# Row buffers, weighing on ScalarE, and the order of the first weights in a four-layer graph kernel on one core

## The reference, cut to what matters

```python
# layer 0: mean over neighbours, then two products and a third of their concatenation
agg = mask @ h / max(deg, 1)
out0 = relu(concat([h @ W_self + b_self, agg @ W_nb + b_nb]) @ W_comb + b_comb)
# layers 1 (8 heads of 64), 2 (4 heads of 128, quaternion weights), 3 (1 head of 512)
Wh = h @ W                                   # rows, one block of columns for each head
e = leaky_relu(f_src[i] + f_dst[j], 0.2)     # f_src, f_dst: one number for each row and head
attn = softmax(where(adj > 0, e, -9e15))
out = attn @ Wh                              # layer 2: elu(out)
```

## Time and profile before

| | us |
|---|---|
| median of three runs | 1111.23 |
| lowest and highest of them | 1106.15, 1111.57 |
| the profiled execution, whole | 1109.11 |
| its span in the trace | 1106.9 |
| busy: TensorE, VectorE, GpSimd, ScalarE | 844.4, 774.2, 634.1, 430.3 |

### The profile page before, as it was taken

One profiled execution on the slowest core, in us unless ns is written; L12 is line 12 of the kernel. 1 busy time (PEld: TensorE's weight loads), 2 busy tenths in 40 slices (PEclk: granted clock), 3 DMA queues, 4 the chain that ended last, 5 costly groups with the idle time before them and its releaser, 6 DMA issues. The chain is left out here.

```text
span 1106.9 us, 11271 instructions
## 1 busy us (share of the span) xinstructions
PE 844.4 (76%) x2786; PEld 471.1 (43%) x2786; DVE 774.2 (70%) x2327; ACT 430.3 (39%) x1277; POOL 634.1 (57%) x636
## 2 busy tenths in 40 slices
PE   0889869999928745959999989467799928876354
PEld 0344434433317534835666646244444523332121
DVE  3899986943349839938689995477899825646374
ACT  3677868111115423624554334355663511110000
POOL 5003401667767777437776730677777057777772
PEclk9999989999959986988999999898999959997767
DMA  9998998938878898647887841678778267776761
GB/s 358 413 395 336 386 393 251 324 104 267 267 248 285 284 233 284 202 153 214 246 245 209 227 128 47 177 232 239 222 211 229 72 155 205 203 206 196 199 189 73
DMA packets 87599, 257.49 MB, mean 233 GB/s; under 512 B 18694, under 2 KB 22182, under 8 KB 83433
## 3 DMA queue, kind: packets, MB, share of 16 engines
q0 software_dynamic: 46896, 157.18, 49.3%
q1 hardware_dynamic: 33116, 85.89, 21.1%
q10 hardware_dynamic: 7516, 13.63, 3.5%
HBM read 209.81 MB, written 53.66 MB: 238 GB/s over the span
## 5 line engine op out<-in xcount | busy, mean ns | idle before, releaser
L1148 POOL DMA_INDIRECT arena<-T,arena x476 | 497.7, 1046 | 266.5 <-issue 202.8
L771 PE MATMUL psum<-arena,misc 128*128 128x512 f32 x408 | 207.3, 630 | 32.9 <-DVE arena L1527 25.4
L747 PE MATMUL psum<-arena 128*128 128x264 f32 (+1 forms) x832 | 207.8, 394 | 0.9 <-ACT arena L869 0.9
L670 PE MATMUL psum<-misc,arena 128*128 128x128 f32 (+1 forms) x520 | 87.3, 294 | 153.6 <-ACT arena L853 93.0
L747 PEld LDWEIGHTS psum<-arena 128*128 128x128 f32 (+1 forms) x832 | 159.5, 195 | 59.3 <-issue 25.6
L1527 DVE TENSOR_TENSOR arena<-arena 128x512 f32<-128x512 f32 x238 | 157.4, 689 | 1.2
L670 PEld LDWEIGHTS psum<-misc,arena 128*128 128x128 f32 (+1 forms) x520 | 65.2, 150 | 198.3 <-ACT arena L853 109.5
L853 ACT ACTIVATE arena<-arena 128x512 f32<-128x512 f32 x104 | 85.0, 818 | 114.8 <-DVE arena L1405 70.0
L822 PE MATMUL psum<-arena 128*128 128x512 f32 (+1 forms) x208 | 110.3, 679 | 19.2 <-ACT arena L866 19.2
L771 PEld LDWEIGHTS psum<-arena,misc 128*128 128x128 f32 x408 | 75.4, 200 | 103.5 <-issue 66.8
L869 ACT ACTIVATE arena<-psum 128x128 f32<-128x128 f32 (+1 forms) x312 | 82.3, 283 | 88.8 <-PE psum L670 88.7
(11 more groups left out here) (143 smaller groups left out, 972.5 us busy)
## 6 DMA issues: line engine op xcount, KB each, us to landing
arena<-in_adj SPq DMA_DIRECT2D x25, 1663.5 KB, 12.4
T<-arena SPq DMA_DIRECT2D x75, 260.0 KB, 3.8
arena<-T,arena POOLq DMA_INDIRECT x476, 4.2
T<-arena ACTq DMA_DIRECT2D x25, 256.0 KB, 9.4
XV<-in_x SPq DMA_DIRECT2D x1, 6400.0 KB, 29.8
XV<-arena ACTq DMA_DIRECT2D x25, 256.0 KB, 3.8
PW<-arena POOLq DMA_DIRECT2D x5, 1024.0 KB, 27.0
arena<-in_x SPq DMA_DIRECT2D x1, 3072.0 KB, 18.7
```

The lines of the kernel that those rows point to most:

```text
L670: last = e.transpose(to[:, k * P:k * P + n], src[0:n, k * P:(k + 1) * P], ident[0:n, 0:n])
L747: last = e.matmul(p_wh[m % 2][0:n, a, :], ht[:, k, 0:n], WL[l][:, k, a, :], start=k == 0, stop=k == 3)
L771: e.matmul(p_num[s % 3].rearrange("p (a o) -> p a o", a=2), ident, halves(GB[:, BASE[l, s] + of[n][0], :])[:, :, 0:HALF], start=n == 0, st ...
L1148: e.indirect_dma_start(GB[:, BASE[l, s] + k, 0:ROW], None, dr["T"][l], bass.IndirectOffsetOnAxis(ap=(IDP if l else IDX)[:, t, k:k + 1], ax ...
```

## The change

Five edits go together.

1. From layer 1 on the rows for the next table lie in four buffers instead of two (`ROWS`: `WO` and the first two of `XV`, which are free by then), and the stores count on four semaphores.
2. In layer 2 ScalarE multiplies the last rows of a tile by their weights (`aid`, after `node_ht` and before `exp` in its round), one [128 x 128] activation for each of the four heads: 4 rows of the tile with 15 slots, 2 of each with 8 or 7, 1 of each with 6, 5 or 4. That is 22 of 119 rows and 88 activations. TensorE waits for them on a semaphore of their own, and VectorE before it overwrites the weights.
3. ScalarE does `turn(0)` between `mark(0)` and `mark(1)`, and `mix(0, 0)` and `mix(0, 1)` between `mark(1)` and `mark(2)`. SyncE issues the second piece of adj ahead of the 2 KB load of b_nb.
4. The five copies into `PW` and that of the bias go from GpSimd's queue to SyncE's, behind the loads of the attention vectors (after the second-last mark) and ahead of the copy of x into `XV`, of the places and of the load of the lists.
5. VectorE's product of 2048 columns (L1353, six times) becomes four of 512.

```diff
+def aided(l, t):
+    return {15: 4, 8: 2, 7: 2, 6: 1, 5: 1, 4: 1}.get(SLOTS[t], 0) if l == 2 else 0
+def aided_ahead(l, s):
+    return sum(aided(i, t) for i in range(1, l + 1) for t in (ORDER if i < l else ORDER[:s]))
...
+    ROWS = WO + [v[:, 0:WIDE] for v in XV[0:2]]
...
+    def row_buffer(l, s):
+        return WO[s % 2] if l == 0 else ROWS[s % 4]
     def wait_stored(e, l, s):
-        e.wait_ge(S[f"stored{s % 2}"], 16 * (l * NT // 2 + s // 2 + 1))
+        e.wait_ge(S[f"stored{s % 4}"], 16 * (l * len(range(s % 4, NT, 4)) + s // 4 + 1))
...
+        load_adj(1)
         e.dma_start(g["bcol"], dr["b_nb"].rearrange("(k p) -> p k", p=P), allow_slow_non_contiguous=True).then_inc(S["bcol0"], 16)
-        load_adj(1)
...
+        for which in range(5):
+            src = (W0[0], W0[1], S2, PB, S1)[which]
+            if which == 0:
+                e.wait_ge(S["bank_out"], bank("mix", 1, 3) + 1)
+            elif which == 2:
+                e.wait_ge(S["w1"], 8 * 16)
+            elif which == 3:
+                e.wait_ge(S["hamilton"], 16)
+            elif which == 4:
+                e.wait_ge(S["bank_out"], bank("turn", 3, 3) + 1)
+            e.dma_start(dr["PW"][which], src.rearrange("p k o -> p (k o)")).then_inc(S[f"pw{which}"], 16)
+        e.wait_ge(S["bias_row"], 1)
+        e.dma_start(dr["PB"], g["brow"][0:1, 0, :]).then_inc(S["pb_out"], 16)
...
-                buf = WO[s % 2]
+                buf = row_buffer(l, s)
...
+            mine = len(of) - aided(l, ORDER[s])
+            if n < mine:
+                e.wait_ge(S["weighed"], units_ahead(l, s) - aided_ahead(l, s) + n + 1)
+            else:
+                e.wait_ge(S["aided"], aided_ahead(l, s) + n - mine + 1)
...
+        turn(0)
         mark(1)
+        for k in range(2):
+            mix(0, k)
         for t in range(NT + 1):
             if t + 2 < NT:
                 mark(t + 2)
             for job in JOBS[t]:
+                if job in (("turn", 0), ("mix", 0, 0), ("mix", 0, 1)):
+                    continue
...
-            if s >= 2:
+            if l == 0 and s < 2:
+                wait_out(e, "vout", NT - 2 + s)
+            elif l == 0:
                 wait_stored(e, l, s - 2)
-            elif l:
-                wait_stored(e, l - 1, NT - 2 + s)
+            elif s >= 4:
+                wait_stored(e, l, s - 4)
+            elif l == 2:
+                wait_stored(e, l - 1, max(i for i in range(NT) if i % 4 == s))
+            elif s < 2:
+                wait_stored(e, 0, NT - 2 + s)
             else:
-                wait_out(e, "vout", NT - 2 + s)
+                e.wait_ge(S["x_new"], NT)
+        def aid(s):
+            j, i, c = SET_OF[2, s]
+            t = ORDER[s]
+            n, NH = SLOTS[t], HEADS[2]
+            if aided(2, t):
+                e.wait_ge(S["normalized"], j + 1)
+            for k in range(n - aided(2, t), n):
+                for h in range(NH):
+                    part = halves(GB[:, BASE[2, s] + k, :])[:, h // 2, h % 2 * P:h % 2 * P + P]
+                    last = e.activation(part, part, ACT.Copy, scale=E[j % 2][:, (i * n + k) * NH + h:(i * n + k) * NH + h + 1])
+                last.then_inc(S["aided"], 1)
...
+                if l == 2 and 0 <= r - 1 < NT:
+                    aid(r - 1)
...
-        def keep(which):
-            src = (W0[0], W0[1], S2, PB, S1)[which]
-            e.dma_start(dr["PW"][which], src.rearrange("p k o -> p (k o)")).then_inc(S[f"pw{which}"], 16)
...
-        keep(0)
-        keep(1)
-        e.dma_start(dr["PB"], whole).then_inc(S["pb_out"], 16)
-        keep(3)
-        e.wait_ge(S["w1"], 8 * 16)
-        keep(2)
         e.wait_ge(S["mark"], NT - 3)
         e.memset(ADJ[(NT - 1) % 3][96:P, :], 0.0).then_inc(S["adjpad"], 1)
-        e.wait_ge(S["bank_out"], bank("turn", 3, 3) + 1)
-        keep(4)
...
-                place(e.tensor_tensor(PA, (S2, PB, S1)[l - 1], AB[n].unsqueeze(1).broadcast_to([P, 4, D]), ALU.mult))
+                for k in range(4):
+                    place(e.tensor_tensor(PA[:, k, :], (S2, PB, S1)[l - 1][:, k, :], AB[n], ALU.mult))
...
+            if l >= 2:
+                before, first, steps = SETS[j - 2]
+                e.wait_ge(S["aided"], aided_ahead(before, first + steps))
...
-            for k, size in units(l, ORDER[s]):
+            for k, size in units(l, ORDER[s])[:n - aided(l, ORDER[s])]:
```

More of the change, by code:

```diff
@@ L609, in sync @@
             for s, t in enumerate(ORDER if l < 3 else []):
-                buf = WO[s % 2]
+                buf = row_buffer(l, s)
                 e.wait_ge(S["row" if l < 2 else "scored_row"], l * NT + s + 1)
                 for q, (a, b) in enumerate(pieces(t)):
-                    e.dma_start(dr["T"][l + 1][t * P + a:t * P + b, :], buf[a:b, 0:ROW]).then_inc(S["stored_end" if q else f"stored{s % 2}"], 16)
+                    e.dma_start(dr["T"][l + 1][t * P + a:t * P + b, :], buf[a:b, 0:ROW]).then_inc(S["stored_end" if q else f"stored{s % 4}"], 16)
             if l < 2:
@@ L769, in sums @@
                     wait_num_read(e, *(divmod(i - 3, NT) if s >= 3 else (l - 1, NT - 1)))
-            e.wait_ge(S["weighed"], units_ahead(l, s) + n + 1)
+            mine = len(of) - aided(l, ORDER[s])
[3 more added lines that the diff above has]
+                e.wait_ge(S["aided"], aided_ahead(l, s) + n - mine + 1)
             e.matmul(p_num[s % 3].rearrange("p (a o) -> p a o", a=2), ident, halves(GB[:, BASE[l, s] + of[n][0], :])[:, :, 0:HALF],
@@ L795, in tensor @@
                 if 0 <= r - 4 < NT and (l == 2 or r - 1 < NT + 1):
-                    node_tr(ORDER[r - 4], (l + 1) * NT + r - 4, None if l == 1 else WO[(r - 4) % 2])
+                    node_tr(ORDER[r - 4], (l + 1) * NT + r - 4, None if l == 1 else row_buffer(2, r - 4))
                 n = len(units(l, ORDER[r - 1])) if r - 1 < NT else 0
@@ L956, in scores_out @@
             e.activation(SM[0:n, 1, t, :], p_sc[0:n, 8:16], ACT.Copy)
-            e.activation(WO[s % 2][0:n, D:ROW], p_sc[0:n, 0:8], ACT.Copy).then_inc(S["scored_row"], 1)
+            e.activation(row_buffer(2, s)[0:n, D:ROW], p_sc[0:n, 0:8], ACT.Copy).then_inc(S["scored_row"], 1)
         def new_h(l, s):
@@ L963, in new_h @@
                 wait_row_free(l, s)
-            node_h(WO[s % 2] if l == 2 else H, ORDER[s], m, small[m % 2][:, 8:9], small[m % 2][:, 9:10])
+            node_h(row_buffer(2, s) if l == 2 else H, ORDER[s], m, small[m % 2][:, 8:9], small[m % 2][:, 9:10])
         def squares(l, s):
@@ L1171, in gpsimd @@
         for l in (1, 2, 3):
-            for s in (NT - 2, NT - 1, STEP_OF_LAST):
+            for s in (NT - 4, NT - 3, NT - 2, NT - 1, STEP_OF_LAST):
                 wait_stored(e, l - 1, s)
```

2 lines of the change are left out of this document (1 added, 1 removed).

## The result

The changed kernel takes 1104.6 us, the median of 12 runs (1100.7 to 1110.6), beside 1111.1 for the kernel before in as many (1106.2 to 1116.4). The ratio is 0.9938, with a 95% interval of 0.9915 to 0.9961: 6.5 to 6.9 us faster, between 4.3 and 9.4. The forecast was 10 us faster, 1101 us, with a range of 1092 to 1113. The time lies in the range and on the forecast's side, 3.6 us above it. The profiled execution has a span of 1102.5 us and takes 1104.3 whole, beside 1106.9 and 1109.11 of before: 4.8 us less.

What follows compares the result with a forecast made beforehand. The prediction took preparation to 250 us, four streams of gathers and the tails between them as the time. Preparation with layer 0 (-2.6) and layer 2 (-6) took 1109.1 to 1100.5 us, stated as 1101, range 1092 to 1113.

Steps and rivals of the forecast that it cites:

- The first term: Preparation and layer 0 up to the end of its `XV` path: net -2.6 us, from -4.6 and +2.
- the second: Layer 2: 6 us shorter, 5.1 at its end and the rest from `new_h` of step 24; bounds +1 and -10.
- The last mark: End of preparation: ScalarE's last mark 4.6 us earlier, from -6.2 for store waits gone and +1.6 for the new early order.
- The lists: GpSimd's 26 list writes after the marks: 8.6 us saved, between 5 and 11; first gather near 237.
- most of it is lost before `XV`: Layer 0: gathers come 13 us earlier but `own_self` only 4.6, so the wait before `XV` grows from 5.6 to about 14.
- The 2 us for a slower `own_self`: TensorE's chain in layer 0: stores landing in 8.5 us beside x's copy slow it by 2 us, bounds 0 and 17.
- The slow rival: Stores beside `PW` copies land in 20 to 25.6 us and `own_self` loses 12 to 17: 1116 us, chance 0.12.
- The stream: Layer 2's gathers: 3.0 us of waits and 1.3 of lengthenings go, so step 23's rows land 4.3 us earlier.
- From there TensorE is the bound.: Layer 2 after step 23's rows land: TensorE's 35 rows, two products of 0.43 us each, set the pace; 0.8 us gained.
- a sign of being wrong: ScalarE's aided activations in layer 2, taken as 0.30 us each, bounds 0.25 and 0.40: wrong if over 0.4 us.
- A second sign: Layer 2, steps 22 to 25: wrong if VectorE or TensorE wait for ScalarE's `exp` or `new_h`.
- layer 2 gives nothing: Rival: layer 2's stall was slack and its tail is TensorE's, so only -2.6 us: 1108 us, chance 0.25.

Runs made afterwards that it cites:

- e2_no_early_order: The changed kernel with ScalarE's old order of the first weights and marks and adj's second piece behind b_nb again: 1101.1 us, 0.9921 of the kernel before.
- e3_whole_products: The changed kernel with VectorE's six products of 2048 columns in one piece again: 1103.75 us, 0.9928 of the kernel before.
- the three and the five kernels above: Three profiled kernels without four row buffers and `aid`; five with four buffers and the old orders, one of them without `aid`: layer 2 took 200.5 and 197.4 us.
- e3_no_aid: The changed kernel with no row weighed on ScalarE, so VectorE weighs all 119 of layer 2: 1103.1 us, 0.9948 of the kernel before.

## Why the prediction was right, and where it wasn't

The forecast's side and range were right. Its sum came out near by luck: -2.6 - 6 was forecast, and -5.0 - 3.1 is what the profiles show together. The first term was too small by 2.4 and the second too large by 2.9, and the two errors nearly cancel. The 8.1 together lie within the interval of the measured 6.9.

**The last mark was right, edit 3's part of it for another reason.** It was forecast for about 182 and starts at 182.15; VectorE's start moved 4.45 us for the 4.6 forecast, and with edit 4 alone 6.9 for the 6.2 (the first list write at 193.40). Edit 3 was set at 1.6 us and costs 2.0 between the means; that the size is near is luck. That nothing was to be gained early was as forecast: adj's pieces land at the same rate, and the mark at 49.40 waits 5.64 us for one. But the cost was to come from VectorE, which would search the third piece 3.4 us later, with 1.8 us of idle time to absorb it. In after it started that search at 31.50, 2.6 us later than before, and went without the 1.77 us of idleness ahead of the fourth; that leaves 0.9 us. Most of the 2 us arises from TensorE's idle spell and lower clock ahead of the seventh mark, shown at e2_no_early_order, which the forecast didn't have.

**The lists were too optimistic, without effect.** The writes save 6.4 of the 8.6 us: the 26 take 4.7 us more than 26 x 0.976 + 25 x 0.30 (11.1 before, not 11.0), where 2.4 was allowed. Nine writes were lengthened by 0.4 to 0.5, where twelve by 0.2 had been allowed for. A product of 512 columns takes 0.686, and a write beside it up to 1.50, so it pays at most about one piece each time. The Trainium skill's rule cited in the prediction (SBUF — State Buffer, "SBUF: two separate sides") is in line with that in both forms, 3.06 beside 2048 columns and 1.50 beside 512. A further 2.1 us went into the wait after the last write (8.23 for 6.11); in the other seven kernels with edit 4 that wait was 6.2 to 9.0, and what sets it isn't shown. So the first gather came at 241.6, not 237.

**That most of it is lost before `XV` was right.** The wait grew to 8.7 us in after and to 7.5 - 12.0 in the others with split products, where 12 to 16 was forecast. e3_whole_products shows the mechanism: edit 5 buys 5.2 us at the first gather. At the `XV` gather 2.3 are left of them (0.6 of it the first list write), within the 307.9 to 311.1 of the four kernels that have edits 3, 4 and 5, and the time shows nothing.

**The 2 us for a slower `own_self` was the failed term of preparation.** Stores were to land in 8.5 us beside x's copy and cost 0.8 for each of five or six tiles. The first four landed in 7.6 to 7.9, the next in 6.4 and less. By the prediction's own formula that is (7.7 + 0.95) / 2 - 3.95 = 0.4 us for each of four tiles, as an estimate, and the two PSUM buffers took most of it: TensorE lost 0.48 us, in two idle spells of 0.30 and 0.18, where it had lost 0.45. In the other seven kernels with edit 4 it lost 0 to 2.2, and in the means nothing is left of it at the first `XV` gather. The slow rival took 20 to 25.6 us from the earlier trace rows and is refuted: the five stores of `own` that were beside the copies of 1 MB from SyncE's queue landed in 7.4 to 9.3. No store of `own_self` was among them; the first was issued at 206.4, when the last copy landed. The DMA engines were as busy there as they had been beside GpSimd's copies (a share of 1.02 from 185.6 to 206.7, and from 120 to 158 before). That the queue makes the difference wasn't tried.

**Layer 2 was half of what was forecast,** and two steps failed.

- *The stream.* 3.0 us of waits and 1.3 of lengthenings were to go, and the last rows to land 4.3 earlier. The waits of the earlier trace rows did go: no gather of layer 2 in after waits over 0.5 us. But GpSimd's busy time rose from 126.0 to 128.7 us, so the stream took 163.9 us instead of 164.2. In the means of the three and the five kernels above busy time rose from 126.8 to 127.9 and the stream went from 165.5 to 163.0, 2.4 us less for the 4.3 forecast, and the scores of step 22 came only 1.0 earlier. With the stalls gone 38 to 43 of the 119 issues still took over 1.0 us, where 41 or 42 had. The 22 products taken off VectorE shortened nothing that can be seen: e3_no_aid, with all 119 of them, has 127.4 us of busy time and after 128.8. That it is VectorE's work that lengthens an issue is argued from the list writes and wasn't tested in layer 2.
- *"From there TensorE is the bound."* TensorE was the bound from 840.8 only, and what held it up was the order of instructions: rows that were ready stood behind scores that waited for rows that had not landed. The prediction's check for it was the wrong one: it looked for TensorE waiting for ScalarE's `exp` and `new_h`, not for VectorE. The trace of before couldn't show the wait itself, since VectorE was late there and the rows had landed (step 22's scores at 140.9 without a wait), but the order was in the code. With the orders changed the tail gives back 2.3 to 2.6 us, of the 2.9 that were missing; in the length of the one layer profiled it doesn't show (196.6 us beside 197.4 in the mean).

**`aid` was costed right as a pace, wrong as a duration.** An activation takes 416 ns from start to end, above the 0.40 named as a bound and as a sign of being wrong, but they overlap: 16 in a row took 4.78 us, 0.30 each. A second sign came too, VectorE waiting for `exp` in steps 24 and 25 (3.46 and 1.57 us), and TensorE for the last `new_h` (0.31 and 0.93). Neither sign meant what it was named for: TensorE's sums went on without a gap, and before the last `new_h` it had waited 1.43 in before.

The Trainium skill, ScalarE: Activation LUTs, section "What ACT_TABLE_LOAD costs", gives 293 ns by the working in the prediction; the trace agrees with the pace of 0.30 us. Nothing hung on it.

Waits for ScalarE were there too, 6.8 us in 10 times for `aid`. It bought nothing that can be told: VectorE, which it relieves, waited 10 us for rows even without it. In the rival "layer 2 gives nothing" it was said that `aid` doesn't matter; that half of the rival came true.

## What to carry to other kernels

When an engine that was late catches up with its data, read its instruction order again: an instruction that waits for data not landed is better placed behind all work whose data has landed, on this engine and on the engine that feeds the next one; here the other order held back 2 to 3 us. Before costing an edit at the head of a chain, find the next wait that two branches share; here 5 us on the branch of the gathers were worth nothing that the time shows, and 7 on that of the marks were worth 6. When an edit moves work forward, look at what the engine does in the place that falls empty: here TensorE stood 15 us, came back at a lower clock, and the edit cost 2 us. And for a term of 3 us compare several profiles of kernels with the same code in that stage, since the same layer took between 195.7 and 199.5 us.

## What the hardware showed unexpectedly

- A 256 KB store from ScalarE's queue landed in 14.3 to 25.6 us from 120 to 151 in before, beside 1 MB copies from GpSimd's queue and adj, and in 7.4 to 9.3 beside five such copies from SyncE's queue with x's copy behind them, at the same share of the DMA engines (1.02). Why is open.
- The 8 products of TensorE after its 10.87 us of idleness took 5.63 us, 0.70 each, and the 30 after them 13.04, 0.43 each. The clock granted to TensorE was 0.65 of full speed in the first stretch, between its levels of 1.2 and 2.4 GHz, and 1.00 in the second; in e2_no_early_order, after 10.24 us of idleness, it was the same. Beyond the stall this cost at most 8 x (0.70 - 0.43) = 2.2 us. Some of it is VectorE's pace: its third row was ready at 836.16, from where the last four products would have ended at 837.9 at 0.43 each, and they ended at 839.69. That leaves 1.8, as an estimate.
- The same program took 105 us more in one series than in the others, with waits for stores of 10 to 20 us that came once layer 0's gathers ran, so that the ranking of the variants was lost. The record gives the same chip number for it as for a series at 1110 us.
